# A two-layer attention and mixture kernel: routing in smaller pieces, and idle-bank products between the gate's tiles

## The reference

```
x = x + attention0(layernorm(x))                  # 16 heads of width 8
x = x + mixture0(layernorm(x)):
    scores = sigmoid(x @ gate_W) * route_scale    # 8 experts
    two largest, divided by their sum             # weights, 0 for the other six
    sum_e weight_e * (gelu(x @ W1_e + b1_e) @ W2_e + b2_e) + a shared expert of the same form
x = x + attention1(layernorm(x))                  # 8 heads, 4 key/value heads, width 128
t = x * rsqrt(mean(x*x) + eps) * scale
g = t @ gate_w.T + gate_b                         # 16 experts, softmax of the four largest
x = x + sum_e route_e * (swiglu(t @ mlp1_e + b) @ mlp2_e + b2_e)
```

## Time and profile before

| | |
|---|---|
| median of 3 runs | 1046.99 us (1046.92 to 1049.65) |
| the profiled execution | 1044.53 us, its span 1042.8 us |
| PE busy | 939.0 us (90%) |
| DVE busy | 728.0 us (70%) |
| ACT busy | 624.1 us (60%) |
| POOL busy | 345.9 us (33%) |
| mean granted TensorE clock | 0.961 of full speed |

### The profile page before, as it was taken

The page is one execution under the profiler, slowest core; times in us unless marked ns, Lnnn a source line. Parts: engine busy times, 40 slices in busy tenths (PEclk is TensorE's granted clock), DMA queues, the critical chain, the costliest instruction groups (busy, mean ns, idle before and its releaser), DMA issues. The chain is left out here.

```text
span 1042.8 us, 16193 instructions
## 1 busy us (share of the span) xinstructions
PE 939.0 (90%) x5608; PEld 538.2 (52%) x5608; DVE 728.0 (70%) x1498; ACT 624.1 (60%) x1245; POOL 345.9 (33%) x385
## 2 busy tenths in 40 slices
PE   3699999999999998895799999999999999889898
PEld 2222323222232323333567676777777676678797
DVE  6889999999999984537345454545454547676776
ACT  3268888888888884322455555555565554355665
POOL 5700000000000000004594847575666653245322
PEclk9689999999999998897799999999999999999999
DMA  3400111110000000000000000000000020000000
GB/s 67 154 27 22 37 54 36 42 32 24 22 20 21 1 2 1 0 1 17 1 11 1 1 6 11 1 2 6 11 1 1 6 82 1 0 2 11 11 12 11
DMA packets 23370, 20.03 MB, mean 19 GB/s; under 512 B 5176, under 2 KB 17440, under 8 KB 23288
## 3 DMA queue, kind: packets, MB, share of 16 engines
q1 hardware_dynamic: 23288, 18.99, 6.2%
HBM read 14.26 MB, written 4.59 MB: 18 GB/s over the span
## 5 line engine op out<-in xcount | busy, mean ns | idle before, releaser
L832 ACT ACTIVATE probs<-score_bank 128x512 f32<-128x512 f32 x512 | 267.9, 601 | 75.3 <-PE score_bank L908 75.1
L698 DVE TENSOR_REDUCE halves<-max_bank 128x2 f32<-128x1024 f32 x256 | 298.4, 1218 | 11.0 <-PE max_bank L868 8.9
L1457 ACT ACTIVATE a_probs<-a_scores,a_lowest 128x896 f32<-128x896 f32 (+7 forms) x128 | 94.9, 742 | 117.5 <-DVE a_lowest L1452 117.0
L1807 PE MATMUL a_sum<-a_turned,a_v 128*128 128x512 f32 (+3 forms) x384 | 158.9, 501 | 1.4 <-ACT a_headsT L1718 1.3
L868 PE MATMUL max_bank<-k_stack,q_stack 48*128 48x512 bf16 x512 | 117.3, 397 | 24.9 <-DVE halves L698 24.7
L921 PE MATMUL summed<-probs,v_tile 128*32 128x512 f32 x1024 | 138.8, 615 | 0.0
L908 PE MATMUL score_bank<-q_stack,k_stack 50*128 50x512 bf16 x512 | 132.6, 386 | 3.7 <-ACT probs L832 2.2
L1452 DVE TENSOR_REDUCE a_lowest<-a_scores 128x1 f32<-128x896 f32 (+7 forms) x128 | 96.1, 755 | 42.1 <-PE a_scores L1446 42.1
L625 POOL COPY v_tile<-values 128x128 f32<-128x128 f32 x16 | 4.6, 294 | 303.3 <-PE summed L921 303.2
L1798 PE MATMUL a_turn<-identity,a_probs 128*128 128x128 f32 x576 | 95.7, 275 | 5.9 <-ACT a_probs L1457 5.4
L1654 DVE COPY a_turned<-a_turn 128x512 f32<-128x512 f32 x96 | 57.4, 598 | 53.5 <-PE a_turn L1798 53.2
(11 more groups left out here) (282 smaller groups left out, 1630.5 us busy)
## 6 DMA issues: line engine op xcount, KB each, us to landing
rope<-in_rope SPq DMA_DIRECT2D x8, 256.0 KB, 3.0
rope<-in_L_ffn_mlp_w SPq DMA_DIRECT2D x8, 256.0 KB, 4.5
q_parts<-l_q_parts SPq DMA_DIRECT2D x2, 768.0 KB, 4.7
k_parts<-l_k_parts SPq DMA_DIRECT2D x2, 768.0 KB, 6.1
q_stack<-q_parts SPq DMA_DIRECT2D x30, 48.0 KB
k_stack<-k_parts SPq DMA_DIRECT2D x30, 48.0 KB
x<-in_L_attn_x SPq DMA_DIRECT2D x2, 512.0 KB, 4.2
q_stack<-shift SPq DMA_DIRECT2D x64, 2.0 KB
```

The source lines that it names most:

```text
L698: dve.reduce_max(halves[:, u % 2, half, :].rearrange("p (x t) -> p x t", x=2)[:, :, qt], max_bank[place % RING][:, :, :], AX_X).then_inc(f ...
L832: act.activation(probs[:, step % PROBS, x, :], score_bank[e % SCORES][:, :], ACT.Exp, scale=SCALE0).then_inc(prob_ready, 1)
L1457: act.activation(probs[:, k % 2, c, 0:row_width(n)], scores[n % 2][:, 0:row_width(n)], ACT.Exp, bias=lowest[:, n % 8:n % 8 + 1], accum_out ...
L1807: pe.matmul(sum_bank[:, skipped(k, j):CH], v[:, BLOCKS[k][0], j, :], turned[:, m % SLOTS, skipped(k, j):CH], start=(j == 0), stop=(TURNED_ ...
```

## The change

It does this, in program order:

- `inverse_root` (first mixture, both batches) makes three steps instead of four.
- The last unit of the first attention makes the gate's eight tiles in two halves of four, the second two score products later, and issues one bf16 product (`fill`) ahead of each tile. A fill multiplies 50 rows of the key and query stacks into the second bank of `max_bank[SPARE]`, which nothing reads. ACT's `score` moves from behind the two exponentials of step 6 to between them, and waits for both halves.
- `mark` and `weigh` of the first batch move from the first mixture's start into the first attention, ahead of the last `divide`.
- In the first mixture `turn_parts(0)` stands ahead of the ups, the inverse root stands ahead of the first `weigh_hidden`, `take_parts(1)` goes behind `weigh_hidden(0, 2)`, PE's transposes stand one or two sums earlier, and the gate is made in two halves. ACT scores after `leave(0)`. DVE ranks ahead of `weigh_hidden(1, 0)`. The fp32 copy of the weights goes to POOL with a semaphore of its own.
- In the second mixture DVE clamps two experts ahead instead of one. Routing work is spread over more units and later ones: moments of two tiles per unit, one root step per unit, marks in two halves. Normalising the second batch's eight rows goes from DVE to POOL, two per unit. In the second attention only the grouping of calls changes.

```diff
-    for _ in range(4):
+    for _ in range(3):
...
+                def fill():
+
+                    rows, stack = slice(0, NST + 2), (NPAIR - 1) % STACKS
+                    pe.matmul(max_bank[SPARE][:, 1, :], k_stack[stack][rows, 0:P], q_stack[stack][rows, 0:CH], start=True, stop=True)
+
+                def score_experts(part):
+                    if part == 0:
+                        pe.wait_ge(mix_in, 16 * 14)
+                        pe.wait_ge(mix_taken, CB)
+                    m0.gate(pe, max_bank[SPARE][:, 0, :], 0, part, fill).then_inc(mix_gate, 1)
...
+                        if e == LAST_AHEAD:
+                            act.wait_ge(mix_gate, 2)
+                            m0.score(act, max_bank[SPARE][:, 0, :], 0).then_inc(mix_scored, 1)
...
                     m0.rank(dve, chain, 0)
+                    m0.mark(dve, chain, 0)
+                    chain.after(m0.weigh(dve, chain, 0))
...
-                    chain.after(dve.tensor_copy(weightT[:, cols], part_bank[:, :]))
-                    dve.tensor_copy(weightT32[:, cols], weightT[:, cols]).then_inc(partT_out, 1)
+                    dve.tensor_copy(weightT[:, cols], part_bank[:, :]).then_inc(partT_out, 1)
...
+                turn_parts(0)
                 for j in range(NU):
                     up(0, j)
-                pe.wait_ge(parts_ready, 1)
-                turn_parts(0)
...
                 dve.wait_ge(prob_ready, 1)
                 m0.rank(dve, chain, 1)
+                weigh_hidden(1, 0)
+                m0.mark(dve, chain, 1)
                 weigh_hidden(1, 1)
-                m0.mark(dve, chain, 1)
+                m0.weigh(dve, chain, 1).then_inc(parts_ready, 1)
                 weigh_hidden(1, 2)
-                m0.weigh(dve, chain, 1).then_inc(parts_ready, 1)
+                take_parts(2)
                 weigh_hidden(1, 3)
                 add(0)
-                take_parts(2)
                 take_parts(3)
...
                 for c in range(1, NCH):
                     leave(c - 1)
+                    if c == 1:
+                        act.wait_ge(gate_ready, 2)
+                        m0.score(act, spare, 1).then_inc(prob_ready, 1)
...
+        STATS_AT = {i: range(TB + 2 * i, TB + 2 * i + 2) for i in range(TB // 2)}
+        AGGREGATE_AT, VALUE_AT, GUESS_AT, ROOT_AT, SECOND_AT = 4, 5, 6, (7, 8, 9), 10
+        ROWS_AT = {11 + i: range(TB + 2 * i, TB + 2 * i + 2) for i in range(TB // 2)}
+        TURN_WEIGHT_AT = {3: 0, 5: 1, 36: 2, 38: 3}
+        TURN_AT, LOWER_AT = {14: 2, 18: 3}, {15: 2, 19: 3}
+        GATE_AT = {20 + i: TB + i for i in range(TB)}
+        BIAS_AT, TOP_AT, MARK_AT, ASK_AT, POWERS_AT, WEIGH_AT = 28, 28, {29: 0, 30: 1}, 31, 32, 33
...
+                    if n in ROWS_AT:
+                        pool.wait_ge(root_found, 1)
+                        for tile in ROWS_AT[n]:
+                            m1.normalise(pool, t.x, tile).then_inc(normed_ready, 1)
...
                 clamp(0)
+                clamp(1)
                 for n in range(N):
                     c, e = divmod(n, UNITS)
-                    if e < E1 and expert(n) + 1 < NCH * E1:
-                        clamp(expert(n) + 1)
+                    if e < E1 and expert(n) + 2 < NCH * E1:
+                        clamp(expert(n) + 2)
```

More of the change, by code:

```diff
@@ L196, in normalise, with gate @@
         return last
-    def gate(self, pe, gate_bank, b):
-        for tile in range(TB):
+    def gate(self, pe, gate_bank, b, part, between=None):
+        for tile in range(part * TB // 2, (part + 1) * TB // 2):
+            if between is not None:
+                between()
             cols = slice((b * TB + tile) * P, (b * TB + tile + 1) * P)
@@ L353, in find_top, with mark @@
         chain.after(dve.tensor_copy(self.wanted[:, of, 0:K1], self.top[:, of, 0:K1]))
[L355 to L356 removed]
+    def mark(self, dve, chain, tiles):
+        for tile in tiles:
             last = dve.match_replace(out=self.marked[:, tile, :], in_to_replace=self.wanted[:, tile, :],
```

110 lines of the change are left out of this document (52 added, 58 removed).

## The result

The changed kernel takes 1035.88 us (median of 4 runs, 1035.67 to 1036.52). The kernel before took 1047.69 beside it (4 runs, 1046.92 to 1049.65). The ratio is 0.9885 with a 95% interval of 0.9868 to 0.9903: 11.8 us faster, of 13.9 forecast, and 2.8 above the forecast time of 1033.1.

What follows compares the result with a forecast made beforehand. PE, busy 90% of the span, was taken to bound the kernel. A to E summed to −13.9 us from the profiled 1044.5, giving 1030.6; 2.5 added back for the median made 1033.1, range 1027.5 to 1039.5.

Steps and rivals of the forecast that it cites:

- rival 1: The fills in the first attention's drain do not keep the clock: median near 1037, chance 0.15.
- the likeliest case: The whole kernel, all terms as summed: median 1033.1 us, chance 0.62.
- A: Drain of the first attention: eight fills, 1.6 us of PE, last divide waits for DVE: +0.8 us, bounds −0.3 and +3.3.
- B: First mixture's start and chunk 0: 20.2 us for 27.9, so −7.7, bounds −9.0 and −4.
- C: First mixture's chunk 1: new waits for ranking and weight copy, 15.1 us for 15.35, so −0.2, bounds −2.5 and +2.
- E: Second mixture's first two chunks: 9.1 us of waits fall to 1.3, so −7.8, bounds −9.1 and −2.
- D: The clock: one more stretch of 2 us at half clock, +1.0 us, bounds 0 and 3.
- The second: Rival: POOL's rows come late in the second mixture, gain there 5 less, about 1038, chance 0.12.
- The third: Rival: ACT held at the table change in the second mixture's unit 32, +2.2 us, median 1035.3, chance 0.05.
- The last two: Rivals: waits in both mixtures only move, 1045 to 1049, chance 0.03; clock stays down in the first mixture, 1067, chance 0.03.
- the fourth: Rival: waits in both mixtures only move to other causes, 1045 to 1049, no change, chance 0.03.

Runs made afterwards that it cites:

- e1: The changed kernel without the eight fills: 1033.17 us, ratio 0.9834.
- e7: e6 with the first mixture's copy of the third chunk's weights behind the eighth multiplication and sum, its transposes after the last sum: 1030.97 us.
- e11: The changed kernel with the second batch's inverse root in the first mixture behind the first multiplication: 1037.34 us, ratio 0.9885.
- e10: e7 with second-mixture row transposes and low parts in units 15 and 18, first batch's weigh back in the first mixture, its transposes behind the ups: 1029.58 us.
- e4: The kernel before with one edit, the second mixture's clamp two experts ahead: 1048.00 us, ratio 0.9977.
- e3: The changed kernel with the second mixture's clamp one expert ahead: 1041.14 us, ratio 0.9908.
- e6: The changed kernel without fills, first-mixture ranking behind the fifth multiplication, second-mixture row transposes in units 15 and 17, low parts in 16 and 18: 1032.82 us.
- e2: The changed kernel with the first mixture's ranking of the second batch behind the fifth multiplication: 1034.05 us, ratio 0.9840.
- e5: The changed kernel repeated unaltered: 1037.00 us, ratio 0.9880.

## Why the prediction was right in the sum, and where it was not

The number lay in the range, but it came there with luck. The measured 1035.88 is nearer to rival 1 (about 1037) than to the likeliest case (1033.1), and it is rival 1's mechanism that came. By the two traces the gain was 8.7 us of the 13.9 forecast: terms A, B, C and E were too kind by 2.4, 1.1, 2.3 and 1.0, of which the clock term D and small differences elsewhere cover 1.6. The medians are nearer, 11.8, since the trace of before that the sum was made against was 3.2 us under its median and that of the changed kernel was not; the 2.5 that I added back for this made up half of the miss. Term by term, against the same two traces:

**A, the drain: forecast +0.8, measured +3.2.** This step failed, at the size of its first term: "they are 1.6 us of PE", from 0.2 for a product of a row of two. Here a fill between the gate's tiles cost some 0.4, and e1 shows 3.0 for the eight. The clock fell as well: the fold took 1.85 where I had put it at full clock with 1.04, a part of what the +3.3 bound stood for. I had also left the last fold at 402.17, as if nothing stood ahead of it on PE. It began 9.3 us after the gate's first tile before and 12.1 after it now, and so I named the wrong engine: the last divide waited 0.34 for PE in the changed kernel, not for DVE. DVE binds only where fold and fills are out of the way, as e7 shows, by 1.2.

**B, the mixture's start and chunk 0: forecast −7.7, measured −6.6.** Chunk 0 by itself was 14.94 for a forecast of 14.9. The ups took 6.4 and not 5.3: the four behind the first took 5.37 in this trace for 4.09 before, at a granted clock of 0.70. The place of the root, which I gave half of the reason, has no part (e11); what counts is that the weights are done before the block, with their transposes ahead of the ups (e10).

**C, chunk 1: forecast −0.2, measured +2.1.** 1.3 for the ranking was 1.64, 1.2 for the copy was 1.10, so both waits were sized well, 2.7 for 2.5. The step that failed is a comparison of unlike clocks. The forecast chunk, 15.1, was summed at full clock; the old one, 15.35, held a stretch at half clock (0.89), and the new one got one too (0.90). At full clock on both sides it is 13.70 (e4) and 15.76 (e3), at the lower clock 15.35 and 17.44: 2.1 more each way. 1.8 of it is what PE waits more (2.74 for 0.95 before). The stretch at half clock, some 1.7 us, is in both traces. At full clock the new chunk is 0.7 above my 15.1: 0.2 in the waits, 0.4 in PE's own work (13.02 in e3 for 12.6).

**D, the clock: forecast +1.0.** It is contained in the measured A, B and C, and can't be told from them. The chunk 1 of before lost as much to the clock as that of now.

**E, the second mixture: forecast −7.8, measured −6.8.** The 9.1 of waits were too many from the start: PE's idle time in the two chunks was 3.73 + 4.02 = 7.75 in the earlier trace rows, and it is 3.06 now, 4.7 less. PE's busy time in them fell by 2.1, of which 1.2 are the two sets of weight transposes that moved to chunk 2; what the other 0.9 is stays open. Three waits or places differ from the forecast. PE waited 1.65 for POOL's rows where I had 0.7. It waited 1.42 at the gate for DVE's low part, which I had not listed, while the late chain of weights, for which I had 0.6, cost nothing. And the last chunk gained 1.1 that I had not seen. Chunk 2 pays for the moved transposes (27.81 for 26.66).

**Rivals.** The first, that the fills do not keep the clock, is what happened, at a part of its price: I gave it 0.15, and it deserved more, as the trace of before held nothing to say that fills would. The second, rows late on POOL, happened at 0.9 us of its 5. The third did not happen: the unit with the two table loads shows no wait of PE. ACT in that unit of the changed kernel:

```profile
976.02 1.28 ACT L377 ACT_TABLE_LOAD   x1
977.58 0.31 ACT L377 ACTIVATE m_powers<-m_weight 128x128 f32<-128x128 f32 x1 [0.27 <-DVE m_weight L368]
...
978.33 1.28 ACT L2017 ACT_TABLE_LOAD   x1
979.63 0.69 ACT L2017 ACTIVATE m_gated<-m_hid,m_b 128x512 f32<-128x512 f32 x1
```

The activation behind the second load starts 0.02 us after its end, so the drain of the Trainium skill (ScalarE: Activation LUTs, What ACT_TABLE_LOAD costs) is again not seen. The last two did not occur, although e10 shows how the fourth could come about: PE waits for the multiplications behind the weights instead of behind the root.

**What stays open.** Whether an edit of the drain could keep the clock at all; no run here did so on purpose. What the three steps of the root, the fp32 copy on POOL and the gate in two halves are worth by themselves; no run has one of them alone. And how much of the 11.8 us lies in the edits of the second attention, where only the grouping of calls changed: from the first mixture's last transposes to the second mixture's first product it took 445.2 before, 443.5 after, and 442.8 to 445.3 in the runs of the changed kernel and its variants, so nothing can be read from it.

## What to carry to other kernels

Before adding work to hold a clock, price it in the place where it will run, between the instructions that it will alternate with, and ask what shows that it holds anything. A wait of PE can cost more than its length, when a stretch at half clock follows it; whether one does has to be read from more than one trace. Here one followed the 1.65 in the first mixture's chunk 1 in five traces of six and the 2.84 in the second mixture in two of two (e6, e7), but none followed the 1.65 and 1.42 in the second mixture in any of five (the changed kernel, e1, e2, e5, e11). Compare two kernels' stages only at like clocks. And slack made on one engine (a clamp two ahead) is spent at the next dependence: each copy or transposition in a table needs as many units behind its maker as PE now runs ahead; here two were enough (low part in 18, gate in 20) and one was not.

## What was not expected of the hardware

- A bf16 product of 50 rows by 512 columns took 0.2 us behind its like and some 0.4 between fp32 tiles of 8 columns (0.64 for the pair, 0.24 for the tile alone).
- The clock fell in the old chunk 1 of the first mixture too (0.50 from 432.8 to 436.1), where PE was busy throughout and had not waited in the chunk; in e4, the same code there, it did not fall.
- The clock fell at the gate or after it whether or not 512-column products stood in it. In e2 it was at 0.50 while they ran, in e7 it was full up to the last fold with no fill at all.
- Executions of one and the same kernel differ by where the clock falls. In the third set the kernel before took 1047.01 us at a mean granted clock of 0.960 and 1054.23 at 0.950, and nine more runs lie between the two. An edit of 1 us can't be read from five runs of this kernel; its window in the trace can.
- A row of 128 by 128 with two operands per partition took 0.89 us on POOL and 0.34 on DVE.
